# A vision tower's attention and expert block: unread products in TensorE's first stage, and three engines' lists written anew

## What is computed

```python
h = tok_ref(x, W)                                   # patches @ W.T
h = concatenate([cls_tok, h], axis=1)
h = h + attn_ref(layernorm(h), ...)
h = h + ffn_ref(layernorm(h), ...)

# attn_ref(x)
g = ln(x, ln1_w, ln1_b)
k, v, sr = g @ Wk.T, g @ Wv.T, sigmoid(g @ Wr.T)
x = x + sr * bi_wkv(decay / T, first / T, k, v) @ Wo.T
g = ln(x, ln2_w, ln2_b)
x = x + sigmoid(g @ Wr_f.T) * (square(relu(g @ Wk_f.T)) @ Wv_f.T)

# ffn_ref(x): 16 experts in 4 groups, best 2 groups, best 4 experts
idx, w = route(x)
moe = sum over chosen e of w_e * ((silu(x @ Wg_e + bg_e) * (x @ Wu_e + bu_e)) @ Wd_e + bd_e)
return moe + shared(x)
```

## Time and profile before

| | |
|---|---|
| median of three runs | 255.41 us |
| the profiled execution, its own time | 255.63 us |
| its span, first to last instruction | 253.5 us |
| TensorE busy | 242.6 us, 96% |
| VectorE busy | 191.4 us, 76% |
| ScalarE busy | 151.0 us, 60% |
| mean granted clock of TensorE | 0.993 |
| unread products in all | 18 (36 instructions), 11.8 us busy |

### The profile page before, as it was taken

The page is one execution under the profiler, slowest core; times in us unless marked ns, Lnnn a source line. Parts: engine busy times, 40 slices in busy tenths (PEclk is TensorE's granted clock), DMA queues, the critical chain, the costliest instruction groups (busy, mean ns, idle before and its releaser), DMA issues.

```text
span 253.5 us, 4370 instructions
## 1 busy us (share of the span) xinstructions
PE 242.6 (96%) x1508; PEld 222.6 (88%) x1508; DVE 191.4 (76%) x490; ACT 151.0 (60%) x311; POOL 17.9 (7%) x29
## 2 busy tenths in 40 slices
PE   8789899899999999999999999999999999999994
PEld 7677477677588899999999999999999999999993
DVE  5489988999989999999797799877323275843442
ACT  2797899978769999735767862335631341232220
POOL 6100302003101000101100001010000010000000
PEclk9997999999999999999999999999999999999999
DMA  6958271100000430000005510000354000014510
GB/s 170 332 176 309 85 243 62 38 0 0 0 3 10 106 94 13 0 3 0 1 11 157 185 43 1 1 3 0 82 173 136 18 3 0 1 40 92 102 33 27
DMA packets 13165, 17.46 MB, mean 69 GB/s; under 512 B 2359, under 2 KB 11224, under 8 KB 13016
## 3 DMA queue, kind: packets, MB, share of 16 engines
q1 hardware_dynamic: 12872, 17.08, 22.7%
q10 hardware_dynamic: 272, 0.11, 0.2%
HBM read 16.20 MB, written 0.99 MB: 68 GB/s over the span
## 4 chain that ended last, share of the span: by engine, by line
PE 73%; ACT 9%; DVE 8%; issue 4%; DMA 3%; SPq 2%; POOL 0%; DVEq 0%; POOLq 0%
PE PA L998 16%; PE PG L978 16%; PE PG L980 11%; PE PF L998 7%; PE PQ L978 4%; PE PQ L980 3%; PE PX L1029 2%; DMA gates<-c_rows 2%; PE PQ L1049 2%; PE PF L988 1%; PE PG L1149 1%; PE PG L1148 1%; DMA gates<-in_w_k 1%; ACT norm L422 1%; PE PF L1013 1%
## 5 line engine op out<-in xcount | busy, mean ns | idle before, releaser
L584 ACT ACTIVATE act<-PG,columns 128x222 f32<-128x222 f32 (+3 forms) x56 | 28.4, 507 | 58.8 <-PE PG L980 55.1
L978 PE MATMUL PG<-stack,hi_egu 128*128 128x222 f32 (+1 forms) x288 | 62.2, 324 | 0.0
L927 DVE SCALAR_TENSOR_TENSOR hid<-PG,columns,act 128x222 f32<-128x222 f32 (+1 forms) x52 | 27.3, 524 | 28.3 <-PE PG L980 24.8
L998 PE MATMUL PA<-w_ed,hid 128*124 128x192 f32 (+1 forms) x240 | 46.3, 328 | 0.4 <-DVE hid L936 0.3
L978 PEld LDWEIGHTS PG<-stack,hi_egu 128*128 128x128 f32 x288 | 45.6, 190 | 0.7 <-DVE hid L927 0.2
L980 PE MATMUL PG<-stack,lo_egu 128*128 128x222 f32 (+1 forms) x192 | 42.7, 304 | 0.0
L998 PEld LDWEIGHTS PA<-w_ed,hid 128*124 128x124 f32 (+1 forms) x240 | 38.5, 183 | 1.2 <-DVE hid L936 1.2
L980 PEld LDWEIGHTS PG<-stack,lo_egu 128*128 128x128 f32 x192 | 31.8, 190 | 0.0
L396 POOL TENSOR_TENSOR rstd<-var,minus_half 112x2 f32<-112x2 f32 (+3 forms) x12 | 13.9, 1156 | 186.8 <-DVE var L671 186.8
L936 DVE TENSOR_TENSOR hid<-hid,gates 128x222 f32<-128x222 f32 (+1 forms) x48 | 21.9, 462 | 1.8 <-DMA gates<-c_rows 0.9
L998 PE MATMUL PF<-w_down,mix_hid 128*124 128x192 f32 (+1 forms) x120 | 22.8, 326 | 0.0
(11 more groups left out here) (248 smaller groups left out, 443.1 us busy)
## 6 DMA issues: line engine op xcount, KB each, us to landing
gates<-in_w_egu SPq DMA_DIRECT2D x6, 512.0 KB, 4.8
gates<-c_rows SPq DMA_DIRECT2D x16, 138.8 KB, 2.9
gates<-c_rows SPq DMA_DIRECT2D x16, 92.5 KB, 2.8
gates<-c_rows SPq DMA_DIRECT2D x16, 83.2 KB, 2.4
w_ed<-in_w_ed SPq DMA_DIRECT2D x1, 1152.0 KB, 8.0
gates<-c_rows SPq DMA_DIRECT2D x16, 55.5 KB, 2.6
gates<-in_w_up SPq DMA_DIRECT2D x2, 384.0 KB, 4.0
pat<-in_patches SPq DMA_DIRECT2D x2, 370.0 KB, 4.1
```

The lines of the kernel that those rows point to most:

```text
L584: nc.scalar.activation(act[128 - gate:128, n % 2, 0:G.n], PG[0:gate, gate_bank(n), 0:G.n], ACT.Silu, bias=bias).then_inc(act_silu, 1)
L927: V_.scalar_tensor_tensor(out, PG[part, 1, 0:G.n], bias, act[part, i, 0:G.n], ALU.add, ALU.mult).then_inc(mul_done, 1)
L978: mm(out, w_hi[:, slot, cols], x[:, p, 0:G.n], start=(p == 0), stop=False, skip_group_check=True)
L998: last = mm(tile_out(P, G, t), src[:, G.ts[t]:G.ts[t] + G.tp], w, start=start and t != 1, stop=stop, skip_group_check=True)
```

## The change

`pe_heat` gets five more unread products: three behind H:tok (`idle0` to `idle2`, without a wait of their own), one behind F0:kt and one behind F0:rt. ScalarE's `x0` step gets a wait for the token copy. The lists of TensorE, ScalarE and VectorE are written anew: in the first stage VectorE's W:k and W:v go behind the first statistics, ScalarE's Z0:x0 and W:rf go ahead of F0:ln1, F1:tok0 ahead of F0:kf, VectorE's W:sgu ahead of F0:sum; halves of the egu pieces go in between group 0's subtractions and group 1's transposes. Behind that most steps change place with a neighbour or a few. The set of steps is the same but for the five. SyncE's and GpSimd's programs are unchanged. The lists are cut to their heads here:

```diff
--- before.py
+++ after.py
@@ -517,6 +517,7 @@
         def act_first_rows(act_e, g):
             G = GROUP[g]
             since(act_e, norm_ready[2], g)
+            act_e.wait_ge(tok_out, at(tok_out, g, 2))
             act_e.wait_ge(rstd_ready[1], at(rstd_ready[1], g, 1))
             for t in range(G.tiles):
                 last = nc.scalar.activation(x1[0:G.tp, t, :], h0[g % 2][0:G.tp, t, :], ACT.Identity,
@@ -1055,6 +1056,9 @@
             pe.wait_ge(tok_out, 1)
             spin()
             yield "tok"
+            for n in range(3):
+                spin()
+                yield f"idle{n}"
             pe.wait_ge(front_step[0], 1)
             spin()
             yield "stats0"
@@ -1070,6 +1074,9 @@
             pe.wait_ge(pool_rstd[1], 1)
             spin()
             yield "rstd"
+            for after in ("kt", "rt"):
+                spin()
+                yield after
             pe.wait_ge(front_step[0], 5)
             spin()
             yield "scan0"
@@ -1283,67 +1290,67 @@
 
 POOL_ORDER = [(1, 0), (1, 1), (2, 0), (1, 2), (3, 0), (2, 1), (1, 3), (3, 1), (2, 2), (3, 2), (2, 3), (3, 3)]
 PE_ORDER = _order(
-    "H:early0 H:early1 H:early2 H:early3 H:early4 F0:tok0 H:early5 H:tok H:stats0 H:stats1 H:aggr H:var H:rstd F0:tr1a",
-    "F0:tr1b F1:tok0 F1:tok1 F0:k F0:kt F0:v F0:rt F0:r H:scan0 H:scan1 H:sb0 H:sb1 H:e1 H:edge F0:sub0 F0:sub1 F0:sub2",
-    "W:egu0a W:egu0b W:egu1a F1:tr1a F1:tr1b W:egu1b W:egu2a F0:o0 F1:k F1:kt F1:v W:egu2b F1:rt F1:r M0:tr2 F2:tok0",
-    "W:egu3a F2:tok1 F1:sub0 M0:rf M0:up0 F1:sub1 M0:up1 M0:mix0 F1:sub2 M0:up2 M0:mix1 M0:up3 M0:mix2 M0:up4 M0:mix3",
-    "M0:up5 W:egu3b M0:mix4 M0:mix5 F2:tr1a W:egu4a W:egu4b F2:tr1b W:egu5a W:egu5b M0:tr3 F1:o0 M0:logits F1:o1 G0:g0",
-    "G0:g1 F2:k G0:v1 G0:g2 F2:kt G0:v2 G0:g3 F2:v D0:cT G0:v3 G0:g4 F2:rt D0:d1 M1:tr2 F2:r G0:v4 G0:g5 D0:d0 M1:rf M1:up0",
-    "D0:d2 D0:d3 M1:up1 M1:mix0 G0:v5 G0:g6 M1:up2 M1:mix1 D0:d4 M1:up3 M1:mix2 F3:tok0 G0:v6 M1:up4 M1:mix3 G0:g7 G0:v7",
-    "D0:d5 D0:d6 G0:g8 G0:v8 M1:up5 D0:d7 G0:g9 G0:v9 F3:tr1a M1:mix4 M1:mix5 D0:d8 F3:tr1b G0:g10 G0:v10 D0:d9 G0:g11",
...
+    "H:early0 H:early1 H:early2 H:early3 H:early4 F0:tok0 H:early5 H:tok H:idle0 H:idle1 H:idle2 H:stats0 H:stats1 H:aggr",
+    "H:var H:rstd F0:tr1a F0:tr1b F1:tok0 F1:tok1 F0:k F0:kt H:kt F0:v F0:rt H:rt F0:r H:scan0 H:scan1 H:sb0 H:sb1 H:e1",
+    "H:edge F0:sub0 F0:sub1 W:egu0a F0:sub2 W:egu0b W:egu1a F1:tr1a W:egu1b F1:tr1b W:egu2a F0:o0 F1:k F1:kt F1:v W:egu2b",
+    "F1:rt F1:r F2:tok0 M0:tr2 W:egu3a F2:tok1 F1:sub0 M0:rf M0:up0 F1:sub1 M0:up1 M0:mix0 F1:sub2 M0:up2 M0:mix1 M0:up3",
+    "M0:mix2 M0:up4 W:egu3b M0:mix3 M0:up5 M0:mix4 F2:tr1a M0:mix5 W:egu4a W:egu4b F2:tr1b W:egu5a W:egu5b M0:tr3 F1:o0",
+    "M0:logits G0:g0 F1:o1 G0:g1 F2:k G0:v1 G0:g2 F2:kt G0:v2 G0:g3 F2:v G0:v3 D0:cT D0:d1 F2:rt G0:g4 M1:tr2 D0:d0 F2:r",
+    "G0:v4 G0:g5 F3:tok0 M1:rf M1:up0 D0:d2 D0:d3 M1:up1 M1:mix0 G0:v5 M1:up2 M1:mix1 M1:up3 D0:d4 M1:mix2 G0:g6 M1:up4",
+    "G0:v6 M1:mix3 G0:g7 G0:v7 D0:d5 G0:g8 D0:d6 G0:v8 M1:up5 M1:mix4 G0:g9 D0:d7 F3:tr1a M1:mix5 G0:v9 F3:tr1b G0:g10",
...
 )
 ACT_ORDER = _order(
-    "W:cls W:k W:v F0:tok0 W:r F0:ln1 Z0:x0 F0:tr1a F0:tr1b W:rf W:up0 W:up1 F0:k F0:kt F0:vt F0:kf F0:v F0:rt",
-    "W:router F1:tok0 F1:tok1 F0:r F0:exps F0:expe W:sgu W:egu0 F0:w0 F0:w1 F0:w2 W:egu1 W:egu2 L:egu0a F0:wr F1:ln1",
-    "L:egu0b L:egu1a F1:tr1a F1:tr1b L:egu1b L:egu2a W:egu3 F1:k F1:kt F1:vt F1:kf F1:v M0:ln2 F1:rt Z1:x0 F1:r F1:exps",
-    "F2:tok0 M0:tr2 F2:tok1 F1:expe F1:w0 L:egu2b M0:rf M0:mix0 W:egu4 F1:w1 M0:mix1 W:egu5 F1:w2 M0:mix2 L:egu3a M0:mix3",
-    "M0:mix4 F1:wr M0:mix5 F2:ln1 L:egu3b F2:tr1a L:egu4a L:egu4b F2:tr1b M0:ln3 M0:tr3 L:egu5a M0:logits Y0:e0 Y0:e1",
...
+    "W:cls W:k W:v F0:tok0 W:r Z0:x0 W:rf F0:ln1 F0:tr1a F0:tr1b W:up0 W:up1 F0:k F0:kt F0:vt F1:tok0 F0:kf F0:v F0:rt",
+    "W:router F1:tok1 F0:r F0:exps F0:expe W:sgu W:egu0 F0:w0 F0:w1 L:egu0a F0:w2 W:egu1 W:egu2 F0:wr L:egu0b F1:ln1",
+    "L:egu1a F1:tr1a L:egu1b F1:tr1b W:egu3 L:egu2a F1:k F1:kt F1:vt F1:kf F1:v M0:ln2 F1:rt Z1:x0 F1:r F1:exps F2:tok0",
+    "M0:tr2 F2:tok1 F1:expe F1:w0 W:egu4 M0:rf M0:mix0 F1:w1 M0:mix1 L:egu2b L:egu3a W:egu5 F1:w2 M0:mix2 M0:mix3 F1:wr",
+    "M0:mix4 F2:ln1 M0:mix5 L:egu3b F2:tr1a L:egu4a L:egu4b F2:tr1b M0:ln3 M0:tr3 L:egu5a M0:logits Y0:e0 Y0:e1 F2:k Y0:e2",
...
 )
 DVE_ORDER = _order(
-    "W:cls W:k F0:stats1 F0:aggr1 F0:var1 W:v F0:ln1 W:r F0:tr1a F0:tr1b W:rf W:up0 W:up1 F0:scan0 F0:scan1 F0:sb",
-    "F0:e1 F1:stats1 F0:edge W:router F0:top0 F0:top1 F0:sa F1:aggr1 F0:ab00 F0:ab01 F0:ab10 F0:ab11 F1:var1 F0:weigh0",
-    "F0:weigh1 F0:own F0:sum F1:ln1 F0:sum2 W:sgu F0:den F0:recip0 F0:recip1 F0:z F1:tr1a F1:tr1b F0:x10 F0:x1 M0:stats2",
-    "M0:aggr2 M0:var2 F1:scan0 M0:ln2 F1:scan1 F1:sb F1:e1 F1:edge F1:top0 F1:top1 F1:sa M0:tr2a M0:tr2b F2:stats1 F1:ab00",
-    "F1:ab01 F1:ab10 F1:ab11 F2:aggr1 F1:weigh0 F1:weigh1 F1:own F2:var1 F1:sum F1:sum2 F2:ln1 F1:den F1:recip0 M0:gated",
...
+    "W:cls F0:stats1 F0:aggr1 F0:var1 W:k W:v F0:ln1 W:r W:rf F0:tr1a F0:tr1b W:up0 W:up1 F0:scan0 F0:scan1 F0:sb F0:e1",
+    "W:router F0:edge F0:top0 F1:stats1 F0:top1 F0:sa F1:aggr1 F0:ab00 F0:ab01 F0:ab10 F0:ab11 F1:var1 F0:weigh0 F0:weigh1",
+    "F0:own W:sgu F0:sum F1:ln1 F0:sum2 F0:den F0:recip0 F0:recip1 F0:z F1:tr1a F1:tr1b F0:x10 F0:x1 M0:stats2 M0:aggr2",
+    "M0:var2 F1:scan0 M0:ln2 F1:scan1 F1:sb F1:e1 F1:edge F1:top0 F1:top1 F1:sa M0:tr2a M0:tr2b F2:stats1 F1:ab00 F1:ab01",
+    "F1:ab10 F1:ab11 F2:aggr1 F1:weigh0 F2:var1 F1:weigh1 F1:own F1:sum F2:ln1 F1:sum2 F1:den F1:recip0 M0:gated M0:h1",
...
 )
```

## The result

The changed kernel takes 258.14 us (median of 6 executions, 256.83 to 259.18) against 255.43 for the kernel before (6, 255.34 to 256.00): a ratio of 1.0104, 95% interval 1.0072 to 1.0136. It is slower, as forecast, but by 2.7 us and not 1.4, and the time lies 0.3 us above the range.

The account below looks back on a forecast made before the run. VectorE's first scan was taken to set the pace up to 36 us, TensorE to bound the kernel from 88 us. Scan +0.3, clock fall +1.4 and lists -0.3 gave +1.4 on 255.41: 256.8 us, range 254.6 to 257.8.

Parts of the forecast that it names:

- +0.3 (scan): First stage: VectorE's first scan starts at about 17.1 instead of 16.79, 0.3 us later, between 0 and +0.8.
- 1.4 (fall): Clock falls in TensorE's hole before group 1's transposes, between 30.5 and 32, costing 1.4 us; bounds 0 and 1.7.
- 0.3 (lists): Rewritten lists behind 36 us give back 0.3 us; bounds -2.47 and +0.6.
- the root and the shift come 0.5 us earlier: Group 0's statistics no longer wait for lo_k, so GpSimd's root and the shift come 0.5 us earlier.
- The run of nine products: TensorE behind H:tok: nine unread products of 0.45 us take 4.0 us, leaving TensorE free at 12.2.
- 0.8 late: Group 0's transposes start at 12.2, not 11.37: 0.4 from the products, 0.4 from x0 and rf.
- The hole itself: TensorE has nothing to issue from 29.4 to 31.6, ahead of F1:tr1a: 2.2 us, with 0.5 us shortly before.
- an earlier sub0 is worth nothing: TensorE's sub0 starts at 22.3 against 23.24; this 1.0 us is worth nothing to VectorE.
- Mostly neighbours change places: Lists behind 36 us: steps mostly swap with neighbours, so the effect was taken as -0.3 us.
- 2: Rival: no clock fall, scan 0.3 late, lists give 0.3 back: 255.4 us, from 254.9 to 256.1; chance 0.27.
- 3: Rival: new lists fill TensorE's holes between 36 and 88, no fall: 254.5 us with half filled; chance 0.16.
- 4: Rival: clock still falls at 18.5, so VectorE's `own` waits about 1.0 us: 256.7 us; chance 0.07.

Follow-up runs that it names:

- e2: Changed kernel with VectorE's W:k and W:v moved behind F0:ln1, so VectorE idles during group 0's root on GpSimd: 257.20 us.
- e13: e2 with Z0:x0 behind F0:ln1 on ScalarE again, W:rf staying ahead: 257.43 us.
- e15: e13 without the three unread products behind H:tok on TensorE: 256.35 us.
- e5: Changed kernel with M3:gated, M3:h1 and group 3's statistics moved back behind S2:s4, X2:x4, S2:s5 on VectorE: 262.38 us.
- e6: Kernel before plus only the unread products behind F0:kt and F0:rt on TensorE: 255.74 us.
- e10: Changed kernel with S2:s4 ahead of M3:gated and M3:h1 on VectorE: 257.33 us.
- e11: Changed kernel with F2:sum ahead of F3:var1 and F3:ln1 behind X0:x7 on VectorE, as before the change: 258.32 us.
- e12: Changed tail with e10's and e11's moves, on the old head plus kt/rt products, W:rf ahead and VectorE's W:v behind F0:ln1: 255.75 us.
- e14: e12 with Y0:e8 ahead of F3:ln1 on ScalarE, as before the change: 254.95 us.
- e1: Changed kernel without the three unread products behind H:tok; those behind kt and rt stay: 259.08 us.
- e4: Changed kernel's lists and five products up to F0:o0, F0:z and F1:k, the old lists behind: 256.80 us.

## Why the prediction was right in its sign and wrong in its size

- **The sum.** Forecast: +0.3 (scan) + 1.4 (fall) - 0.3 (lists) = +1.4. Measured, without a fall: +1.09 up to F1:k and +1.21 behind it. The fall, in two executions of six, adds 0.3 to the median (258.14 against 257.81). That the sign came out right is luck: without its fall the forecast was no change, and the four executions without one are 2.4 us slower than the kernel before.
- **First stage, forecast +0.3 at the first scan, measured +1.11** (17.90 against 16.79; +1.26 for the stage, counted from the variance). The step that failed is "the root and the shift come 0.5 us earlier". I took the root at its old length; with lo_k moved behind the variances it ran beside lo_k and lo_v and took 1.66 us, so the shift came at 10.27, 0.44 later than before. I had looked at lo_k's queue alone, not at what runs beside the root; e2 puts 0.51 on that. The rest is a late start: the statistics did begin right behind the tokenizer's last product (7.14 against 7.10), as forecast, but that product ended 0.24 later than in the old page, and the variance only 0.17 earlier. The run of nine products was sized well: with the root repaired the transposes start at 12.29 (e2; forecast 12.2) and the scan at 17.28 (forecast 17.1). Only the shares of its "0.8 late" were wrong, 0.4 for the products and 0.4 for x0 and rf: the longer of the two sets the time. With the root repaired, the products alone hold 0.75 (e13), and without them 26.84 is left (e15), 0.14 under the old head.
- **The fall, forecast +1.4.** The place (ahead of F1:tr1a) and the size came out (1.37 in e5's page; 1.26 between after's two kinds of executions, which no page places). What failed is that I took it for certain: the profiled execution has the hole, 0.49 + 1.68 us, and no fall, and two of six have one. I had also read the fall at 18.5 in one page as the kernel's own; it is in few of its executions, so that the clock stayed up there after the change says little. By the gap rule of the Trainium skill that I weighed ("TensorE: Matmul & The Clock Gate", section "HAM oscillation — how this bites in real kernels") this hole would never lower the clock. e5's page, where it does behind 1.68 us, does not agree; the profiled execution of after does.
- **The hole itself** came, and smaller: forecast 2.2 us behind 0.5, from 29.4 to 31.6; measured 1.68 behind 0.49, from 30.71 to 32.39. That lo_sgu ahead of group 1's shift is its cause is not shown. The shift was ready at 30.83, but ScalarE, busy without a break from the third weight (27.84) to the norm (30.93), could not have started the norm sooner in its order either; that weight came 1.04 later than before, since half of egu0 now stands between the subtractions on TensorE. No run separates the two. VectorE lost nothing: from the first scan to the end of z it took 17.46 us, 17.47 before. That an earlier sub0 is worth nothing was right, but after does not show it, since sub0 came at 23.09 there, hardly earlier than 23.24; e6 does, with sub0 at 21.86 and the same first stage.
- **The lists behind 36 us, forecast -0.3 with a bound of +0.6, measured +1.21.** "Mostly neighbours change places" was the failed step. I bounded it by holes on TensorE between 36 and 88, where nothing changed in sum (2.55 us against 2.47), and did not look for instructions with a wait that moved ahead of one that TensorE needs. There are two: M3:gated ahead of S2:s4 (a hole of 1.21; the swap gives back 0.35 to 0.63, e10) and F3:ln1 ahead of S0:s7 on VectorE (a hole of 0.43). Taking the second away gave nothing back (e11) until Y0:e8 went ahead of F3:ln1 on ScalarE too, which is worth 1.0 in the tail and 0.8 in the median (e12 to e14); moving Y0:e8 alone was not tried. F3:tok0 did not fill 84:88 either: 3.40 there against 3.74.
- **Rivals.** 2 had the clock right in four executions of six, and fell with 3 over the lists; 4 fell with the clock at 18.5. None had both halves late.

## What to carry to other kernels

When an instruction that waits is moved up, list what stands behind it on its engine and who needs that, on every engine whose order was rewritten; this tail's loss of 1.2 us lay in two such places in lists that were rewritten throughout. A step put back on one engine needs its readers put back too (e5, e11). Two delays of one instruction are a maximum, not a sum: taking one away shows nothing until the other is gone (e1, e13, e15). One page is one execution: see how often the others have its fall of the clock before counting on it. Keeping the clock up is worth what the slow stretch cost on the path, which here was nothing at 18.5 and 1.37 us at 32.

## What the runs showed of the hardware

- **GpSimd's root beside VectorE.** With VectorE idle the root takes 1.02 us (e2). With lo_k and lo_v running it took 1.66 (1.65 in e4), with F2:sum 2.01, and it ended 0.88 us after lo_v's end (8.94 + 0.42 = 9.36, root 10.24) and 0.87 after F2:sum's (103.57, 104.44). Those operations read two operands from SBUF, and they were not slowed: lo_k took 0.69 us beside the root and 0.68 in e2 without it. The Trainium skill, "SBUF — State Buffer", section "Who interferes with whom", says that such a VectorE instruction contends with a GpSimd instruction that reads SBUF. The trace agrees for these two roots. It does not always: in the kernel before, group 3's root (102.82, 1.01 us) kept its length while VectorE ran such an operation from 103.00 on:

```profile
103.00 1.30 DVE L770 TENSOR_TENSOR E<-E,mx 128x1110 f32<-128x1110 f32 x1
```

  There the root began first. But in after it also began (8.58) ahead of lo_v (8.94) and still waited for it, so what decides is open.
- **The clock is not a function of the hole's length.** Behind a hole of 1.68 us after one of 0.49 us, in the same code, it fell in e5's page and stayed up in after's.
